# Two graph-attention layers and an eight-expert feed-forward: last expert round written out, last weight unit in two transfers

## The reference

```python
x = x + gnn(layernorm(x), edge_index, W1[768,6144], a_src1, a_dst1, b1, W2[6144,768], a_src2, a_dst2, b2)
h = gelu(einsum('bnd,edh->ebnh', x, W1[8,768,3072]) + b1)
y = einsum('ebnh,ehd->ebnd', h, W2[8,3072,768]) + b2
ffn_out = einsum('ebnd,bne->bnd', y, comb)          # comb: the one best expert, times its probability
v = clip(ffn_out @ Wv + bv, -3, 3)
gr, gi = bk_gii(v)       # diagonal of (T - i I)^-1, T tridiagonal with diagonal v: a_i = d_i - 1/a_(i-1), both ways
feats = clip(stack([gr, gi]) * mask, -10, 10)       # mask: the 12 best scores
x = x + ffn_out + bk_scale * (feats @ Wo + bo)
```

## Time and profile before

| | us |
|---|---|
| median of three runs | 492.02 (489.75 to 492.37) |
| the profiled execution | 489.61 |
| its span, first to last instruction | 487.8 |
| last weight unit landed | 464.0 |
| last product with it done | 466.2 |
| output transfer issued | 485.1 |

### The profile page before, as it was taken

How to read it: one execution, slowest core, us unless ns; L and a number is a source line. 1 busy time by engine, 2 the same in 40 slices (tenths; PEclk the granted TensorE clock), 3 DMA queues, 4 the chain that set the end, 5 groups by cost and what they waited for, 6 DMA issues and landing times.

```text
span 487.8 us, 5909 instructions
## 1 busy us (share of the span) xinstructions
PE 461.4 (95%) x2292; PEld 230.0 (47%) x2292; DVE 127.0 (26%) x341; ACT 63.8 (13%) x123; POOL 33.4 (7%) x50
## 2 busy tenths in 40 slices
PE   7999999999999999999999999999999889779882
PEld 5666666666557344344344344344344234224352
DVE  7474676425206320010020010010010001001255
ACT  2101222002003130020020020020020020002200
POOL 3432220000100000000310000000000000000000
PEclk9999999999999999999999999999999999999996
DMA  8989999999999999999999999999999999999900
GB/s 309 403 261 400 403 400 419 415 400 412 423 426 412 367 398 422 426 425 421 407 418 425 423 427 427 421 425 426 423 423 426 427 423 423 426 427 423 388 1 32
DMA packets 32460, 190.04 MB, mean 390 GB/s; under 512 B 5446, under 2 KB 5558, under 8 KB 18108
## 3 DMA queue, kind: packets, MB, share of 16 engines
q1 hardware_dynamic: 31580, 189.74, 94.9%
q0 software_dynamic: 576, 0.06, 0.1%
q10 hardware_dynamic: 288, 0.03, 0.0%
HBM read 189.42 MB, written 0.39 MB: 389 GB/s over the span
## 4 chain that ended last, share of the span: by engine, by line
PE 71%; DMA 14%; SPq 8%; DVE 4%; issue 1%; ACT 0%; DVEq 0%
PE ps L1341 18%; PE ps L1314 17%; PE ps L1093 13%; PE ps L1133 11%; DMA extra<-in_L_ffn_W 7%; DMA lower<-in_L_ffn_W 6%; SPq L332 6%; SPq L327 3%; PE ps L1327 2%; PE ps L1121 2%; PE ps L1269 2%; PE ps L1148 2%; PE ps L1404 1%; DMA x_sb<-in_x 1%; PE ps L1059 0%
## 5 line engine op out<-in xcount | busy, mean ns | idle before, releaser
L1093 PE MATMUL ps<-slot,xT 128*128 128x384 f32 x192 | 64.1, 488 | 0.2 <-ACT xT L490 0.2
L1314 PE MATMUL ps<-extra,gathered 128*64 128x512 f32 x252 | 56.7, 597 | 4.9 <-DMA extra<-in_L_ffn_W 4.9
L1133 PE MATMUL ps<-slot,eluT 128*128 128x384 f32 x168 | 55.3, 486 | 0.0
L1314 PE MATMUL ps<-left,gathered 128*64 128x512 f32 x216 | 49.3, 597 | 3.8 <-DMA left<-in_L_ffn_W 3.3
L896 DVE TENSOR_TENSOR hidden<-ps,b_T 128x384 f32<-128x384 f32 x32 | 16.9, 554 | 122.9 <-PE ps L1327 122.9
L1093 PEld LDWEIGHTS ps<-slot,xT 128*128 128x128 f32 x192 | 35.5, 190 | 23.1 <-ACT xT L490 0.5
L1341 PE MATMUL ps<-lower_2nd,hidden 128*64 128x384 f32 x252 | 43.2, 490 | 2.5 <-DMA lower_2nd<-in_L_ffn_W 2.5
L1133 PEld LDWEIGHTS ps<-slot,eluT 128*128 128x128 f32 x168 | 31.5, 190 | 20.7
L1341 PE MATMUL ps<-lower,hidden 128*64 128x384 f32 x216 | 36.8, 489 | 1.3 <-DMA lower<-in_L_ffn_W 1.0
L1341 PE MATMUL ps<-lower_on,hidden 128*64 128x384 f32 x216 | 37.5, 492 | 0.0
L1314 PEld LDWEIGHTS ps<-extra,gathered 128*64 128x64 f32 x252 | 17.0, 136 | 39.1 <-issue 29.9
(11 more groups left out here) (321 smaller groups left out, 337.0 us busy)
## 6 DMA issues: line engine op xcount, KB each, us to landing
slot<-in_L_gnn_W SPq DMA_DIRECT2D x31, 1152.0 KB, 14.8
extra<-in_L_ffn_W SPq DMA_DIRECT2D x21, 1536.0 KB, 19.5
left<-in_L_ffn_W SPq DMA_DIRECT2D x18, 1536.0 KB, 21.2
lower_2nd<-in_L_ffn_W SPq DMA_DIRECT2D x21, 1152.0 KB, 22.0
lower<-in_L_ffn_W SPq DMA_DIRECT2D x18, 1152.0 KB, 10.5
lower_on<-in_L_ffn_W SPq DMA_DIRECT2D x18, 1152.0 KB, 23.9
chunk<-in_L_ffn_W SPq DMA_DIRECT2D x9, 1536.0 KB, 9.9
lower_extra<-in_L_ffn_W SPq DMA_DIRECT2D x7, 1152.0 KB, 21.0
```

Of the source, the lines that this page charges most:

```text
L1093: last = T.matmul(ps[:, 2 * (h % 2) + b, 0:HB], xT[:, 3 * half + k, :], slots[n % RING][:, k, b * HB:(b + 1) * HB], start=(n % 2 == 0 and ...
L1133: last = T.matmul(ps[:, b, 0:HB], elu_part(KT * h + 3 * half + k, 1)[:, 0, :], slots[n % RING][:, k, b * HB:(b + 1) * HB], start=(h == 0 a ...
L1314: last = T.matmul(ps[b * CAP:(b + 1) * CAP, s, 0:BANK], gathered[:, k, :], upper_homes[k][:, at:at + BANK], start=(k == 0), stop=(k == KT ...
```

## The change

There are three edits.

First, the eighth round is written out. TensorE's loop covers rounds 2 to 6; after it stands `round_(7, last_round=True)`, and then an `If` with the whole code of a ninth round, which is jumped over when there are 8 rounds. On SP the loop covers rounds 3 to 6, and the transfers of round 7 stand behind it. Its last unit of 1152 KB is issued as two transfers into the same home, the slices k = 0 and 1 (768 KB) and the slice k = 2 (384 KB). The second has a semaphore of its own, `last_in`, for which TensorE waits only ahead of the last slice.

Second, the scale factors of the chunk vectors come from the four vectors at the starts of the groups and no longer from all 16. They are taken ahead of and between the products that spread the starts.

Third, 8 fillers stand between the small products L1440 and L1443, and 3 between L1445 and L1448.

```diff
-WARM = (5, 0, 2, 8, 2, 0, 1, 3, 2, 0, 2, 12)
+WARM = (5, 0, 2, 8, 2, 0, 1, 3, 2, 0, 2, 12, 8, 3)
...
-            with sp.Fori(3, ROUNDS) as r:
+            with sp.Fori(3, ROUNDS - 1) as r:
                 load_round(r, r)
+            load_round(ROUNDS - 1, ROUNDS - 1, end=LOADS - 1)
+            sp.wait_ge(used, used_after(ROUNDS - 2) + LOADS)
+            end_unit = w2[ROUNDS - 1, HID - HB:HID, :].rearrange("(p k) c -> p k c", p=P)
+            sp.dma_start(lowers_on[DOWN - 1][:, 0:2, :], end_unit[:, 0:2, :]).then_inc(moe_in[LOADS - 1], 16)
+            sp.dma_start(lowers_on[DOWN - 1][:, 2:3, :], end_unit[:, 2:3, :]).then_inc(last_in, 16)
...
-            for c in range(GC - 1):
-                last = V.tensor_tensor(cf_sx[:, :, c], mm[:, :, 0] if c == 0 else cf_pre[:, c],
+            def spread_start(c):
+                return V.tensor_tensor(cf_sx[:, :, c], mm[:, :, 0] if c == 0 else cf_pre[:, c],
                                        starts[:, :, 0].unsqueeze(2).to_broadcast([2, GC, 4, 4]), ALU.mult)
-            step(last)
+
+            V.tensor_reduce(cf_n[:, :], starts[:, :, 0], AX, ALU.max, apply_absolute_value=True)
+            spread_start(0)
+            step(spread_start(1))
+            V.reciprocal(cf_n[:, :], cf_n[:, :])
+            step(spread_start(2))
             step(V.reduce_sum(starts[:, :, 1:GC].rearrange("p g c a -> p g (c a)"),
                               cf_sx[:, :, :, :, :].rearrange("p g c a b -> p g (c a) b"), AX))
-
-            step(V.tensor_reduce(cf_n[:, :], cf_s[:, :, :], AX, ALU.max, apply_absolute_value=True))
-            step(V.reciprocal(cf_n[:, :], cf_n[:, :]))
-            V.tensor_tensor(cf_s[:, :, :], cf_s[:, :, :], cf_n[:, :].unsqueeze(2).to_broadcast([2, CH, 4]),
-                            ALU.mult).then_inc(cf_ready, 1)
+            V.tensor_tensor(cf_s[:, :, :].rearrange("p (g c) a -> p g (c a)", g=GC),
+                            cf_s[:, :, :].rearrange("p (g c) a -> p g (c a)", g=GC),
+                            cf_n[:, :].unsqueeze(2).to_broadcast([2, GC, 4 * GC]), ALU.mult).then_inc(cf_ready, 1)
...
+                            if last_round and i == DOWN - 1 and k == 2:
+                                pe.wait_ge(last_in, 16)
...
-            with pe.Fori(2, rounds) as r:
+            with pe.Fori(2, ROUNDS - 1) as r:
                 round_(r)
+            round_(ROUNDS - 1, last_round=True)
+            with pe.If(rounds > ROUNDS):
+                round_(ROUNDS)
+            pe.end_ifs()
...
+            stay_warm(WARM[12], 0)
             pe.wait_ge(cf_ready, 3)
...
+            stay_warm(WARM[13], 0)
             pe.wait_ge(cf_ready, 4)
```

More of the change, by code:

```diff
@@ L132, in gnn_moe_kernel @@
               ("cf_m", [CP, CH, 16]), ("cf_mm", [2, CH, 16]), ("cf_s", [2, CH, 4]), ("cf_x", [2, 4, 4]),
-              ("cf_n", [2, CH]), ("cf_p", [CP, CH, 4]), ("cf_b", [CP, 4]), ("cf_y", [CP, CL + 1, 2, 4]),
+              ("cf_n", [2, GC]), ("cf_p", [CP, CH, 4]), ("cf_b", [CP, 4]), ("cf_y", [CP, CL + 1, 2, 4]),
               ("cf_th", [CP, CL + 1, 2]), ("cf_q", [CP, 3, CL, 2]), ("cf_r", [CP, CL]), ("cf_a", [CP, CL, 2]),
@@ L235, in gnn_moe_kernel @@
         second_in = [sem(f"second_in{i}") for i in range(LOADS)]
+        last_in = sem("last_in")
         up_done = sem("up_done")
@@ L332, in load, with load_round @@
                     sp.dma_start(lower_homes[i - CHUNKS][:, :, :], view).then_inc(landed[i], 16)
-            def load_round(r, e, first=0):
-                for i in range(first, LOADS):
+            def load_round(r, e, first=0, end=LOADS):
+                for i in range(first, end):
                     sp.wait_ge(used, used_after(r - 1) + i + 1 - first)
@@ L1293, in first_ffn, with round_ @@
                         pe.wait_ge(b2_added, n + 1)
-            def round_(r, first=False, second=False):
+            def round_(r, first=False, second=False, last_round=False):
                 upper_homes, lower_homes = ((chunks, lowers) if first else (chunks_2nd, lowers_2nd) if second
```

## The result

The changed kernel takes 492.94 us (median of 20 executions) against 491.76 us for the kernel before on the same chips. The ratio is 1.0036, with a 95% interval of 1.0021 to 1.0050: slower, by about 1.8 us. The prediction had 490.5 us and a range up to 492.8. (One execution of each kernel, of 1222 and 799 us, is left out of the ratio; the medians move by 0.2 us at most without them.)

The account below looks back on a forecast made before the run. The end was taken as set by weight bytes up to 464.0 us, TensorE's last-unit work and a serial tail; -0.73 - 0.21 - 0.15 + 0.4 + 0.25 = -0.44 us on 490.9 gave 490.5 us, range 488.2 to 492.8.

Parts of the forecast that it names:

- The split: Last weight unit in two transfers: the last product ends earlier, -0.73 us, bounds -0.73 and 0.
- rival D: At the last unit, the split does nothing: +0.3 us, 491.2 us; chance 0.08.
- The 2 us: Fixed cost per transfer; in series for the last unit's second part it would turn -0.73 into more than +1 us.
- The vectors: Chunk vectors' scaling in the tail: two DVE steps leave the serial end, -0.21 us, bounds -0.25 and 0.
- The instruction packets: Written-out round's code fetched in round 7 may delay weight units: +0.4 us, bounds 0 and +1.1, twice for two packets.
- The jump: TensorE skipping the ninth round's code behind the last matmul: 0 to 0.55 us, taken as +0.25.
- rival B: Written-out code, by jump or packets, costs more than the split gives: +0.5 us, +1.6 with a second packet; chance 0.17.
- The cover: Time from TensorE reaching the branch to the first tail product being due, hiding the jump's fetch: 1.75 us.
- The fillers: 8 and 3 fillers in the tail keep the clock up for L1448: -0.15 us.
- rival C: The 8 tail fillers run at half clock, L1443 starts 1.6 us late: total +1.3 us, 492.2 us; chance 0.05.
- The base: Time of the kernel before, as mean of two middle executions among four: 490.9 us.
- the sign: Whole kernel forecast faster: the sum of all terms was -0.44 us.

Follow-up runs that it names:

- e1: Kernel before with only the last unit's split into two transfers, kept in the loop: 490.71 us, 0.9985 of the kernel before.
- e4: Changed kernel with the body of TensorE's If cut from a whole ninth round to one filler, so a short jump: 490.63 us, 0.9976 of the kernel before.
- e2: Kernel before with only the eighth round written out and the ninth behind an If: 493.80 us, 1.0035 of the kernel before.
- e5: Changed kernel with the x additions and last scatter moved behind the product of the chunk matrices: 495.36 us, 1.0095 of the kernel before.
- e3: Changed kernel without the new 8 and 3 fillers: 493.47 us, 1.0039 of the kernel before.
- e9: Kernel before with split, vectors and written-out last round, the jump ahead of that round, no new fillers: 491.36 us, 1.0001 of the kernel before.
- e8: Kernel before with the split in the loops, the vectors by group and the 8 and 3 fillers: 491.46 us, 0.9995 of the kernel before.
- e6: Kernel before with only the new 8 and 3 fillers added: 492.12 us, 1.0017 of the kernel before.
- e10: Whole changed kernel, fillers included, with the jump moved ahead of the last round: 491.66 us, 0.9997 of the kernel before.
- e7: Kernel before with the split in the loops and the vectors by group, no new fillers: 491.02 us, 0.9986 of the kernel before.
- e11: Kernel before with the split in the loops and the vectors by group, run again: 490.61 us, 0.9988 of the kernel before.

## Why the prediction was wrong, point by point

**The split: right in size, wrong in worth.** -0.73 us was worked out and -0.73 us measured, in the changed kernel and in e1. The step that didn't hold is that a product which ends earlier starts the tail earlier: behind the jump the tail starts when the branch ends, 3.4 to 4.0 us after the sequencer reached it, whatever the products do. In its outcome this is rival D, by a mechanism that I hadn't thought of there. The 2 us that I took from the Trainium skill (DMA: Bandwidth & Descriptors, Anatomy of one DMA) that section gives for the path of transfers issued by GpSimd; here SP issues them, and the unit's last packets end at 465.1 us, 0.5 us ahead of the branch.

**The vectors: right.** -0.21 forecast, -0.26 and -0.27 measured.

**The instruction packets: no cost found.** I gave them +0.4 us. There are 14 packets and not 10, and one of them runs at about 449 us, in the round in which I had put it, but the units behind it are waited for 0.54 and 0.72 us as before, and e4, which has 12 packets, is the fastest of all. It is the lower bound, 0, that held.

**The jump: this is the step that failed.** I took +0.25 us, with bounds 0 and 0.55. Measured are +0.64 (e2), +1.40 (changed), +1.56 (e5) and +1.96 (e3). The mechanism was named, in the sum and as rival B, but its upper end was not an upper end: I used the 2.3 us of the output transfer, counted from the branch, as all that it takes. The branch takes 3.35 us (e2), 3.38 (changed), 3.54 (e5) and 3.94 (e3); the packet starts only 1.0 us into it (1.6 in e3) and takes about 1 us itself. The cover was sized about right, 1.75 us forecast and 2.03 measured after the change (465.59 to 467.62, where L1432 was due); 3.43 us from the branch's start to the product, less 2.03, is the 1.40. In e2, without the split, the cover is 2.76 us: what the split gains in the products it takes from the cover, and 1.40 - 0.64 = 0.76 is just that. I also read the rule of the Trainium skill (Runtime: NRT & Kernel Launch, Instruction fetch mechanics) too strictly. By its figures two loaded pages of 256 instructions can hold the target of a jump over 400, so the rule didn't make the stall certain, and e9 has such a jump without one.

**What was missing: the clock behind the idle time.** I had read in the earlier trace rows that the clock falls after TensorE had done little, and used it for L1448 alone. The same reading belongs to every gap that the change makes. In the profile after, the 2.06 us gap is followed by half the clock, and this costs 2.75 us, more than the gap. It is not in each execution: over the 19 executions up to 496.17 us the mean granted clock goes from 0.982 to 0.994, and correlates with the time at -0.78. But in e2 and e3, which lose as much, the correlation is only -0.42 and -0.38, and e2 has executions of 490.79 and of 495.42 us at 0.988 and 0.989. The 2.9 us between the changed kernel and e4 are about 1.4 us of stall, and the remaining 1.5 us is what I put down to the clock; this split is worked out from one profile and was not measured by itself. A branch that takes longer in the executions that weren't profiled would do it too (it took from 3.35 to 3.94 us in four profiles), and no run decides between the two.

**The fillers: rival C was underrated, and judged by a single row.** I gave them -0.15 us with 0.05 for the rival. In the profile after they overran by 1.28 us (1.6 was the rival's price), in e8 by 0.39 and 0.44; in e4, e6 and e10 not at all. Over executions only e6 shows a cost, 0.17% with an interval from 0.01%; e8 is 0.1% over e7 and e10 level with e9, inside their intervals, and e3 shows no gain from their absence. The row on which I relied, a clock of 1.00 at 478 us, is one execution's, and stands behind 12 fillers that had run mostly at half the clock and ended just in time.

**The base.** I took 490.9 us from four executions; the kernel before has 491.8 here. Of the 2.4 us between 490.5 and 492.94, 0.9 come from this. With it the range would have reached 493.7 and held the time, but the sign was wrong too: -0.44 us forecast, +1.2 by the medians and +1.8 by the ratio.

## What to carry to other kernels

A written-out copy of a loop's body costs little until a jump over it stands on the serial path and lands on code that isn't there. Look up how long the branch itself takes in the trace: 0.2 to 0.4 us here where the code was there, 3.4 to 3.9 where it had to come. A jump right behind the loop was of the first kind here, one behind the written-out round of the second. Or keep the loop. Before paying for a rewrite, ask whether the gain needs it; here the split worked in the loop. And each new gap of a microsecond or two on TensorE is priced with what runs behind it at half the clock, above all where its block and another engine's chain are equally long; fillers that end just in time at the full clock are late at half.

## What was unexpected in the hardware

The jump over some 400 instructions at the end kept TensorE's branch busy for 3.35 to 3.94 us (e2, changed, e5, e3), with a packet on the instruction queue 1.0 to 1.6 us after its start; the short one of e4 took 0.21 us. A jump over the same 400 or so right behind the loop took 0.35 and 0.36 us (e9, e10) and no packet, and the loop's own branches back took 0.21 to 0.26 us. The clock doesn't follow the length of a gap alone: 2.62 us idle in e3 left it at 1.00, 2.06 us after the change brought it to 0.50 for 6.8 us, and 2.38 us at a round's start brought it down in e9, as in e1 and e8 without a jump, and not in e11.
